# Second attention: one score product of 96 stacked rows in place of three, stacked by DMA

## The reference, cut to what matters

```python
# first attention (L0): 32 heads of 128, with a position bias and a mask
score = einsum('bqhd,bkhd->bhqk', h_q, h_k) + position_bias
attn  = einsum('bhqk,bkhd->bqhd', softmax(score), h_v);  out = attn @ w_out.T
# second attention (L1): 32 query heads in 8 key/value groups, head size 16
q = (queries @ Wq).reshape(b, s, 8, 4, 16)
k = (keys @ Wk).reshape(b, s, 8, 16);  v = (values @ Wv).reshape(b, s, 8, 16)
scores = einsum('bqhgd,bkhd->bhgqk', q, k) / 4
out = einsum('bhgqk,bkhd->bqhgd', softmax(scores), v).reshape(b, s, 512) @ Wo
```

## Time and profile before

| | us |
|---|---|
| median of 3 runs | 1857.78 (1857.41 to 1859.46) |
| the profiled execution, whole | 1858.16 |
| its span in the profile | 1856.2 |
| PE busy in the span | 1786.5 (96%) |
| DVE busy | 1414.3 (76%) |

### The profile page before, as it was taken

How to read it: one execution, slowest core, us unless ns; L and a number is a source line. 1 busy time by engine, 2 the same in 40 slices (tenths; PEclk the granted TensorE clock), 3 DMA queues, 4 the chain that set the end, 5 groups by cost and what they waited for, 6 DMA issues and landing times. The chain is left out here.

```text
span 1856.2 us, 29556 instructions
## 1 busy us (share of the span) xinstructions
PE 1786.5 (96%) x10312; PEld 1504.4 (81%) x10312; DVE 1414.3 (76%) x2854; ACT 650.3 (35%) x1783; POOL 672.8 (36%) x453
## 2 busy tenths in 40 slices
PE   8999999999999999997998998879999999999998
PEld 6888889889988889986875665675888888888886
DVE  7767777777777777776546867879788888888886
ACT  5432232123333223224025765530343433343333
POOL 6643343444443333332150003434443333243331
PEclk9999999999999999999999998989999999999999
DMA  4111101111111110111010002010111110111011
GB/s 173 62 51 51 51 23 49 36 45 51 51 51 51 51 48 24 34 40 59 2 46 20 1 26 69 24 64 1 46 35 35 34 35 33 34 34 36 32 35 46
DMA packets 32026, 78.27 MB, mean 42 GB/s; under 512 B 4096, under 2 KB 10944, under 8 KB 31584
## 3 DMA queue, kind: packets, MB, share of 16 engines
q1 hardware_dynamic: 31968, 77.50, 12.8%
HBM read 75.39 MB, written 2.10 MB: 42 GB/s over the span
## 5 line engine op out<-in xcount | busy, mean ns | idle before, releaser
L658 POOL TENSOR_TENSOR l0x_comb<-l0x_neg,l0x_bias 128x1024 f32<-128x1024 bf16 x32 | 69.0, 2155 | 371.8 <-DVE l0x_probs L1056 358.5
L950 ACT ACTIVATE l0x_probs_t<-bank 128x512 f32<-128x512 f32 x32 | 19.1, 597 | 500.6 <-PE bank L795 500.6
L2910 POOL TENSOR_TENSOR l3x_q<-l3x_q,l3x_cross 128x512 f32<-128x512 f32 x64 | 89.8, 1407 | 187.9 <-DVE l3x_q L1881 187.9
L39 PE MATMUL bank<-l0x_w_v_hi,ctx_lo 128*128 128x256 f32 x512 | 144.9, 283 | 0.0
L37 PE MATMUL bank<-l0x_w_v_hi,ctx_hi 128*128 128x256 f32 x512 | 144.9, 283 | 0.0
L38 PE MATMUL bank<-l0x_w_v_lo,ctx_hi 128*128 128x256 f32 x512 | 144.9, 283 | 0.0
L934 ACT ACTIVATE l0x_probs<-l0x_probs,l0x_top 128x129 f32<-128x129 f32 x256 | 99.4, 390 | 53.3 <-DVE l0x_top L1060 53.3
L3097 ACT ACTIVATE l3x_probs<-l3x_probs,l3x_top 128x128 f32<-128x128 f32 x256 | 99.1, 389 | 38.1 <-DVE l3x_top L3178 38.0
L37 PE MATMUL bank<-ctx_hi,l0x_w_k_hi 128*128 128x512 f32 x256 | 104.0, 406 | 7.7 <-DVE ctx_lo L1138 7.7
L1100 DVE TENSOR_TENSOR x<-x,bank 128x512 f32<-128x512 f32 x120 | 82.1, 684 | 37.4 <-PE bank L39 37.4
L37 PE MATMUL bank<-l3x_qin_hi,l3x_w_q_hi 128*128 128x512 f32 x256 | 105.2, 411 | 2.2 <-ACT l3x_v L3131 1.9
(11 more groups left out here) (488 smaller groups left out, 5330.4 us busy)
## 6 DMA issues: line engine op xcount, KB each, us to landing
l0x_raw_k<-L_k_dram SPq DMA_DIRECT2D x32, 256.0 KB, 3.4
l0x_raw_v<-L_v_dram SPq DMA_DIRECT2D x16, 512.0 KB, 3.3
l0x_raw_q<-L_q_dram SPq DMA_DIRECT2D x16, 512.0 KB, 4.3
l0x_raw_o<-L_o_dram SPq DMA_DIRECT2D x16, 512.0 KB, 3.4
l3x_raw<-L_q_dram SPq DMA_DIRECT2D x16, 512.0 KB, 3.3
l3x_raw<-L_o_dram SPq DMA_DIRECT2D x16, 512.0 KB, 3.3
kv_raw<-L_kv_dram SPq DMA_DIRECT2D x8, 512.0 KB, 3.4
l0x_ctx_raw<-ctx_t_dram SPq DMA_DIRECT2D x4, 512.0 KB, 5.3
```

The source lines that it names most:

```text
L39: return pe.matmul(out, lhs[1], rhs[0], start=False, stop=stop)
L658: pool.tensor_tensor(comb[:, :, :], neg[:, :, :], bias[:, j:j + 1, :].to_broadcast([P, B, P]), ALU.add).then_inc(comb_ready, 1)
L950: act.activation(probs_t[:, 0:BH, :], bank[6][:, :].rearrange("p (b n) -> p b n", b=BH), ACT.Copy).then_inc(t_act, 1)
L2910: pool.tensor_tensor(dst[:, part], dst[:, part], cross[n][:, :], ALU.add).then_inc(rotated, 1)
```

## The change

Three groups of edits.

1. **Second attention, scores.** Queries' and keys' parts are stacked in rows. For each quad j of two key groups (32 rows of q), a stationary tile `stack` of 96 rows holds queries high, low, high, and `kd` holds keys high, high, low, each row block with its own group's keys and zeros elsewhere. One matmul of 96 rows x 256 columns (2 groups x 128 keys) makes the sum of the three part products. A unit has four of them in place of six. GpSimd's mask and multiplications are gone. In their place GpSimd and VectorE set `kd` to zero, 24 DMAs from SP copy the keys, and 12 DMAs for each batch copy the queries (for batch 0, 12 for each of its four units, each round after the one before has landed). A second `stack` buffer lies where a weight was kept.
2. **Second attention, order.** ACT's `query_high(1, .)` now comes before `copy_probs`, and DVE's `query_low(1, .)` one unit later.
3. **First attention.** `scores` waits for each half by itself; in the last period `rank_round` 6 and `rank_end` move from before `last_step` to behind `normalise`, DVE's `copy_probs` moves ahead of the maximum, and the heads' high parts go from DVE to ACT, ahead of the exponentials.

```diff
@@ first attention @@
-                def scores(h, j, needed):
-                    pe.wait_ge(ring_drained, needed)
+                def scores(h, j, first_half, both):
                     wait(pe, scores_read, 2 * h)
                     for half in range(2):
+                        pe.wait_ge(ring_drained, both if half else first_half)
...
-                    scores(h, 0, 8 if first else at(p - 1, "k_even1") + 1)
+                    if first:
+                        scores(h, 0, 7, 8)
+                    else:
+                        scores(h, 0, at(p - 1, "k_even1") + 1, at(p - 1, "k_even1") + 1)
...
-                    scores(h + 1, 1, at(p, "k_odd") + 2)
+                    scores(h + 1, 1, at(p, "k_odd") + 1, at(p, "k_odd") + 2)
...
                     copy_probs(h)
+                    if last:
+                        heads_high(h, 0)
                     exps(h + 1, 1)
...
-                            rank_round(p - 1, 3 + m)
-                        rank_end(p - 1)
+                            if m < 3 or not last:
+                                rank_round(p - 1, 3 + m)
+                        if not last:
+                            rank_end(p - 1)
...
-                    add_bias(LAST, 1)
-                    copy_probs(LAST - 1)
-                    for half in range(2):
-                        dve.wait_ge(h_full, 2 * (LAST - 1) + half + 1)
-                        dve.tensor_copy(heads[0][:, 0, half * HALF:(half + 1) * HALF], bank[6 + half][:, :]
-                                        ).then_inc(h_hi, 1)
+                    add_bias(LAST, 1, lambda: copy_probs(LAST - 1))
                     heads_low(LAST - 1, 0)
                     normalise(LAST, 1)
+                    rank_round(N - 2, ROUNDS)
+                    rank_end(N - 2)
                     copy_probs(LAST)
@@ second attention: SP @@
                 sp.dma_start(raw[:, :, :], dram["L1x_wq"]).then_inc(raw_loaded, 16)
+                sp.wait_ge(kd_zero, 2)
+                sp.wait_ge(kt_done, 2)
+                for s, part in enumerate(KEY_PARTS):
+                    for j in range(QUADS):
+                        for m in range(2):
+                            head = slice(j * ROWS + m * HD, j * ROWS + (m + 1) * HD)
+                            sp.dma_start(as_f32(kd[s * ROWS + m * HD:s * ROWS + (m + 1) * HD, j, m, :]),
+                                         as_f32(kt[part][head, :])
+                                         ).then_inc(kd_done, 16)
                 sp.wait_ge(w_ready, 1)
                 sp.wait_ge(raw_loaded, 16)
                 sp.dma_start(raw[:, :, :], dram["L1x_wo"]).then_inc(raw_loaded, 16)
+                def stack_queries(b, units):
+                    for s, part in enumerate(PARTS):
+                        for j in range(QUADS):
+                            sp.dma_start(as_f32(stack[b % 2][s * ROWS:(s + 1) * ROWS, units, j, :]),
+                                         as_f32(q[part][j * ROWS:(j + 1) * ROWS, units, b * P:(b + 1) * P])
+                                         ).then_inc(stacked[b % 2], 16)
+                for g in range(G):
+                    sp.wait_ge(q_done, g + 1)
+                    wait(sp, stacked[0], LANDED * g)
+                    stack_queries(0, slice(g, g + 1))
+                sp.wait_ge(vt_full, 2)
+                stack_queries(1, slice(0, G))
+                for b in range(2, B):
+                    if b == BH:
...
+                        ffn.load(sp)
+                    sp.wait_ge(s_full, G * (b - 1))
+                    stack_queries(b, slice(0, G))
@@ GpSimd @@
+                pool.memset(as_f32(kd[:, 0:QUADS - 1, :, :]), 0.0).then_inc(kd_zero, 1)
                 split_low(0, w_q)
                 pool.memset(v[:, :, :, :], 1.0).then_inc(filled, 1)
-                        pool.tensor_tensor(kd[s][:, :, half_of(half)],
...
@@ PE @@
-                    for n, (ql, kl) in enumerate(((0, 0), (1, 0), (0, 1))):
-                        for r in range(ROW_TILES):
-                            rows = slice(r * ROWS, (r + 1) * ROWS)
-                            mm = pe.matmul(bank[2 * (u % 2) + r][:, :].rearrange("p (m k) -> p m k", m=BH),
-                                           q[ql][rows, g, tokens], kd[kl][rows, :, tokens], start=n == 0, stop=n == 2)
+                    if b == 0:
+                        pe.wait_ge(stacked[0], LANDED * (g + 1))
+                    elif g == 0:
+                        pe.wait_ge(stacked[b % 2], LANDED * (b // 2 + (G if b % 2 == 0 else 1)))
+                    for j in range(QUADS):
+                        mm = pe.matmul(bank[2 * (u % 2) + j // 2][:, j % 2 * 2 * P:(j % 2 + 1) * 2 * P]
+                                       .rearrange("p (m k) -> p m k", m=2), stack[b % 2][0:STACK, g, j, :],
+                                       kd[0:STACK, j, :, tokens], start=True, stop=True)
@@ ACT and DVE @@
+                    if u == 0:
+                        query_high(1, 0)
+                    if 2 <= u <= G:
+                        query_high(1, u - 1)
                     if u >= 1:
                         copy_probs(u - 1)
-                    if u < G:
-                        query_high(1, u)
...
+                dve.memset(as_f32(kd[:, QUADS - 1, :, :]), 0.0).then_inc(kd_zero, 1)
...
-                    if u < G:
-                        query_low(1, u)
+                    if 1 <= u <= G:
+                        query_low(1, u - 1)
```

More of the change, by code:

```diff
@@ L86, in keep_kv @@
     def keep_kv(self, ctx):
-        self.sb(ctx, "l1_wkv_kept", [P, 2, DC * 2 * P])
+        self.stack_kept = self.sb(ctx, "l1x_stack1", [P, 4, 4, P], F32R)
     def statistics(self, dve, b):
@@ L1048, in _, with add_bias @@
             def _(dve):
-                def add_bias(h, j):
+                def add_bias(h, j, ahead_of_top=None):
                     dve.wait_ge(comb_ready, h + 1)
@@ L1057, in add_bias @@
                                           comb[:, part, :], ALU.add).then_inc(scores_read, 1)
+                    if ahead_of_top:
+                        ahead_of_top()
                     dve.wait_ge(scores_read, 2 * h + 2)
@@ L1317, in l1_layer @@
     KV, G, HD = L1_GROUPS, L1_QUERIES, L1_DIM
-    ROWS, COLS = 64, 32
-    ROW_TILES, COL_TILES = P // ROWS, P // COLS
+    COLS, COL_TILES = 32, 4
+    QUADS, ROWS, PARTS, KEY_PARTS = 4, 32, (0, 1, 0), (0, 0, 1)
+    STACK = ROWS * len(PARTS)
+    LANDED = 16 * QUADS * len(PARTS)
     UNITS = B * G
@@ L1331, in l1_layer @@
         q = core.cin
-        kd = pair("kd", [P, BH, T])
+        kd = sb("kd", [P, QUADS, 2, T], F32R)
         w_o = pair("w_o", [P, G, D])
@@ L1342, in l1_layer @@
         a, at = sb("a", [P, G, KV, HD]), pair("at", [P, G, P])
-        same, select = sb("same", [P, KV]), sb("select", [P, BH])
         top = [sb(f"top{n}", [P, KV]) for n in range(2)]
         xn, w_q, raw = sb("xn", [P, B, D]), pair("w_q", [P, DC, D]), sb("raw", [P, DC, D])
+        stack = [sb("stack0", [P, G, QUADS, P], F32R), core.stack_kept]
         ffn.norm.claim()
-        made, same_ready, select_ready = sem("made"), sem("same_ready"), sem("select_ready")
-        filled = sem("filled")
+        filled, kd_zero, stacked = sem("filled"), sem("kd_zero"), [sem("stacked0"), sem("stacked1")]
         kt_full, kt_hi, kt_done, kd_done = sem("kt_full"), sem("kt_hi"), sem("kt_done"), sem("kd_done")
@@ L1373, in _ @@
                 sp.dma_start(raw[:, :, :], dram["L1x_wo"]).then_inc(raw_loaded, 16)
-                sp.wait_ge(q_full, 2 * G)
-                sp.wait_ge(w_ready, 2)
-                ffn.load(sp)
+                def stack_queries(b, units):
[12 more added lines that the diff above has]
+                    if b == BH:
+                        sp.wait_ge(q_done, 2 * G)
+                        sp.wait_ge(w_ready, 2)
+                        ffn.load(sp)
+                    sp.wait_ge(s_full, G * (b - 1))
+                    stack_queries(b, slice(0, G))
                 sp.wait_ge(s_full, UNITS)
@@ L1384, in _ @@
             def _(pool):
[L1385 to L1393, removed]
                 pool.wait_ge(core.var_done, n_power + 1)
@@ L1510, in _ @@
                 pe.wait_ge(core.xt_copied, B * n_norm + B)
-                pe.wait_ge(kd_done, 2)
+                pe.wait_ge(kd_done, 2 * LANDED)
                 pe.wait_ge(q_done, 2)
@@ L1529, in _ @@
                         pe.wait_ge(q_done, 2 * G)
-                        pe.wait_ge(kd_done, 4)
                         pe.wait_ge(w_ready, 2)
@@ L1717, in _ @@
                 dve.wait_ge(filled, 1)
-                dve.wait_ge(kd_done, 4)
+                dve.wait_ge(kd_done, 2 * LANDED)
                 for u in range(UNITS):
```

## The result

| | before | changed |
|---|---|---|
| median of 5 runs, us | 1858.3 (four of them 1857.41 to 1859.46) | 1878.76 (1876.16 to 1881.66) |
| ratio, 95% interval | | 1.0107 (1.0092 to 1.0122) |
| span of the profiled execution, us | 1856.2 | 1874.2 |
| PE busy in it, us | 1786.5 | 1779.6 |

A forecast was written before the change was run, and what follows sets the result against it. PE, busy 96% of the span, was taken as the bound. Terms -1.35 - 5.9 - 4.4 + 9.7 + 1.0 = -0.95 gave 1857.2 on the profiled execution, forecast 1856.8 us; 8-in-10 range 1848 to 1868.

The forecast's parts named there:

- First attention, start and end (-1.35, -5.9): First attention: PE's waits for queries and keys shrink, 1.35 us; at its end idles shrink and clock stays up, 5.9.
- GpSimd's memset, costed at 0: Second attention's start: zeroing the keys takes 5.5 us but ends before the copies could start, so 0.
- The rival: Second attention's start: GpSimd's memset blocks DVE's normalisation, 5.2 to 12.8 us, time 1862.0 to 1869.6; chance .22.
- The issue distance, 0.512: SP's queue, second attention's start: each issue 0.512 us after the last, the mean of nine in a row.
- T4: Second attention's start: time of unit 4's scores, 954.15 + 81 p + 8.15, forecast at 1003.7.
- p: SP's queue: the distance of two issues, taken as 0.512 us; the number that rests on least.
- more slowly, p = 0.6: Rival, SP's copies issued more slowly: 1863.9 us; chance .14 together with no steady gain.
- Units 4 to 7 in 10.4: Second attention's start: units 4 to 7 run free at a quarter batch each, 3 x 3.47 = 10.4 us.
- the new order of the query parts: Second attention's start: `query_low` behind the next unit takes 0.7 from each of four units, under SP's rounds: 0.
- Steady state -4.4: Second attention's steady batches: two of four units' scores count, 0.73 us saved per batch over six batches, -4.4.
- The clock's +1.0: Second attention's start: PE idles in each copy round, so its clock falls to 0.50, +1.0 us (0 to 3).

The follow-up runs named there:

- l0_order: Kernel before plus the first attention's edits and only the second attention's new order of query parts, on the old scores: 1846.74 us, ratio 0.9939.
- no_lock_one_round: Changed kernel with GpSimd's memset held until VectorE's normalisations are done and batch 0's queries stacked in one round of 12: 1852.39 us, ratio 0.9969.
- issue_probe: Kernel before plus five series of eight unneeded copies on SP, three inside the chip, two from DRAM: 1861.04 us in a single run.
- best_b: Changed kernel, ScalarE zeroing the key tile, high keys copied first, batch 0 in two rounds, low parts issued from GpSimd's queue: 1843.97 us, ratio 0.9930.

## Why the prediction was wrong

- **First attention, start and end (-1.35, -5.9): right.** The profile has -1.5 (PE's first transposes of probabilities start at 55.40 in place of 56.94) and the other -5.9 of the 7.4. The wait for l0x_q went, the clock stayed up, and the rank round was hidden. One working in it does not give its number: (1030.60 - 1029.70) / 4 divides the time of three pairs by four. The 0.22 to 0.23 at the higher level is right all the same: after the change 17 of PE's projection matmuls in a row stand (840.74 - 837.08) / 16 = 0.23 apart.
- **GpSimd's memset, costed at 0: the first step that failed.** I said "both end before the copies could start: 0" and looked only at who waits for the memset. It takes 5.23 us, as forecast, but VectorE is held. The rival named it, with 5.2 to 12.8 us; measured 10.8 in the normalisation, +10.6 alone in the kernel before, -10 when moved. I gave it .22 though the trace had it on a line of sixteen instructions, 277 ns against 2484, and my counter-argument, that a memset reads nothing, rested on no row. What I wrote at the beginning, that the engines meet only at semaphores, is not so here: no semaphore stands between the memset and the normalisations. The rule of the Trainium skill, SBUF — State Buffer, section "SBUF: two separate sides", which the rival named, says that of a VectorE instruction in a two-port mode and a GpSimd instruction whichever starts first gets the shared ports for its whole instruction. The trace agrees: GpSimd's memset starts at 939.13, VectorE's first normalisation at 939.21, and that one stands 5.43 us.
- **The issue distance, 0.512: the second step that failed, by size.** T4 = start + 81 p + 8.15 was the right formula: with p = 0.635 and the first copy at 957.11 it gives 957.11 + 81 x 0.635 + 8.15 = 1016.7, measured 1016.58. But the 0.512 was the mean of ten loads from DRAM that stand 0.38 to 0.63 apart. Inside the chip it is 0.62 to 0.69. 81 x 0.123 = 10.0 us. The case "more slowly, p = 0.6" had the mechanism at .14 together with another.
- **Units 4 to 7 in 10.4: 9.8 measured (1016.58 to 1026.40), and in part luck.** I had it from the steady batch, and put the new order of the query parts at 0. But it is this order that makes it possible, and it is worth 6 us alone: on the old scores the stretch goes from 18.2 to 11.8. Where PE does not stand in front of unit 4, the steady batch is not met: it is 11.8 in l0_order and 1001.34 - 990.02 = 11.3 in no_lock_one_round.
- **Steady state -4.4: right in kind, too large.** -3.4 measured. The doubled scores show that two of four units count. The four matmuls cost 1032.94 - 1032.34 = 0.60 and 1037.40 - 1036.73 = 0.67, not 0.48 and 0.57, so that the two save 0.29 + 0.23 = 0.52, and the batch is 14.59 - 14.02 = 0.57 shorter, not 0.73.

The key copies began 957.11 - (954.15 - 7.25) = 10.2 later than forecast; with the 10.0 of the issues that is 20.2 us. The steady state adds 1.0. The clock's +1.0 goes: the clock was low, 0.74 from 980 to 1008, but there PE stood waiting for copies, and no cost of it shows apart. With the quicker units 4 to 7 that gives back 1.6. On the profiled execution, for which the sum had 1857.2, this makes 1857.2 + 19.6 = 1876.8, measured 1876.16. The median of the runs, 1878.76, lies 2.6 above that execution, and no row shows why. Both failures point the same way, and the range, which held each alone, did not hold both: 1868 was the end of either.

## What to carry to other kernels

Look at what a new piece of GpSimd work runs beside, not only at who waits for it: here 5 us of a memset that nobody was waiting for cost 10, because what it held then met the next works of GpSimd. When a copy inside the chip replaces arithmetic, count its issues before its bytes, on the queue they stand in: four rounds of twelve small copies cost 16 us more than one round of twelve large ones. And of a change in several parts, time the parts alone: the order of the query parts, a side issue here, carried 6 us, more than the new score product.

## What the runs showed of the hardware

- An issue on SP took 0.62 to 0.69 us for a copy inside the chip, whether it moved 1 row or 128, and 0.46 to 0.55 for the two shapes from DRAM in issue_probe; among the ten loads from DRAM in the kernel before it was 0.38 to 0.63.
- GpSimd's queue issued eight key copies in 4.09 us, 0.51 each, with VectorE's work beside them. SP's sixteen, of which the later ones stood beside these, took 10.93 us in place of 10.08 (best_b):

```profile
951.60 4.09 POOL L1440 DMA_DIRECT2D l1x_kd<-l1x_kt_lo  x8
```

```profile
946.24 10.93 SPq L1387 DMA_DIRECT2D l1x_kd<-l1x_kt_hi  x16
```

- VectorE, once held, does not always get its turn between two GpSimd instructions. In the gap of 0.33 us behind the memset it did (944.56); but the normalisation that began at 945.01 stood through the change from GpSimd's work of 944.69 to that of 949.39 and ended only at 951.48.
